# A wait ahead of every indirect transfer of the first layer

## The reference

```python
residual = x
xn = _layernorm(x, ln_g, ln_b)
abel = gelu(xn @ aw1 + ab1) @ aw2 + ab2                       # dense, hidden width 512
nonabel = _rotate(_moe(xn, gate_w, gate_b, ew1, eb1, ew2, eb2), gens)  # top 2 of 6 experts, width 256
gate = sigmoid(concat([abel, nonabel]) @ gc_w + gc_b)
return residual + abel * (1 - gate) + nonabel * gate
```

## Time and profile before

| what | value |
|---|---|
| median of 3 runs | 826.95 us (826.12 to 827.61) |
| the profiled execution's own time | 825.18 us |
| its span in the profile | 823.5 us |
| PE busy | 654.0 us, 79% |
| DVE busy | 500.6 us, 61% |
| ACT busy | 398.7 us, 48% |
| POOL busy | 388.6 us, 47% |
| TensorE's mean granted clock | 0.902 |

### The profile page before, as it was taken

One profiled execution on the slowest core, in us unless ns is written; L12 is line 12 of the kernel. 1 busy time (PEld: TensorE's weight loads), 2 busy tenths in 40 slices (PEclk: granted clock), 3 DMA queues, 4 the chain that ended last, 5 costly groups with the idle time before them and its releaser, 6 DMA issues.

```text
span 823.5 us, 19422 instructions
## 1 busy us (share of the span) xinstructions
PE 654.0 (79%) x6221; PEld 464.7 (56%) x6222; DVE 500.6 (61%) x1349; ACT 398.7 (48%) x1102; POOL 388.6 (47%) x523
## 2 busy tenths in 40 slices
PE   5978776742688208888956899999899999989894
PEld 3766555641587208756744355545599974444442
DVE  5787432730466006529885887878644457767784
ACT  3433231201344004447751667877644446766794
POOL 6352863067401750068630366753333327766682
PEclk9998886985799658999966999999999999999998
DMA  8990111011356324311100000000022211111110
GB/s 240 305 291 1 36 42 39 1 48 55 66 104 107 70 52 88 84 39 30 26 11 26 15 22 26 28 28 2 9 63 70 70 34 40 34 31 31 27 28 26
DMA packets 69465, 48.33 MB, mean 59 GB/s; under 512 B 8011, under 2 KB 63750, under 8 KB 69382
## 3 DMA queue, kind: packets, MB, share of 16 engines
q1 hardware_dynamic: 62332, 34.09, 16.6%
q0 software_dynamic: 6144, 12.63, 5.6%
q10 hardware_dynamic: 906, 0.55, 0.2%
HBM read 24.00 MB, written 23.24 MB: 57 GB/s over the span
## 4 chain that ended last, share of the span: by engine, by line
PE 47%; issue 14%; DVE 11%; POOL 10%; another core or an unknown queue 7%; DMA 6%; ACT 3%; SPq 0%; DVEq 0%; POOLq 0%; ACTq 0%
PE bank L1640 8%; DMA xg<-x_half 5%; PE bank L1599 4%; PE bank L1692 4%; PE bank L1701 4%; POOL vs L1550 4%; PE bank L1061 3%; PE bank L1625 3%; PE bank L1047 3%; POOL xn_all L1529 3%; PE bank L1026 2%; PE bank L1016 2%; PE bank L535 2%; PE bank L518 1%
## 5 line engine op out<-in xcount | busy, mean ns | idle before, releaser
L1760 ACT ACTIVATE pb<-bank,nmx 128x512 f32<-128x512 f32 x256 | 173.4, 690 | 65.8 <-DVE nmx L1891 65.5
L1891 DVE TENSOR_REDUCE nmx<-bank 128x2 f32<-128x1024 f32 x128 | 154.9, 1215 | 6.7 <-PE bank L1640 6.0
L1640 PE MATMUL bank<-qk 64*128 64x512 f32 x512 | 131.4, 623 | 8.1 <-ACT pb L1760 5.7
L1550 POOL TENSOR_TENSOR vs<-vt,rz 128x256 f32<-128x256 f32 x128 | 78.6, 616 | 119.4 <-DVE rz L1867 117.0
L1108 ACT ACTIVATE turns<-bank,cols 128x128 f32<-128x128 f32 x148 | 46.6, 365 | 111.9 <-PE bank L1016 49.2
L345 POOL DMA_INDIRECT x_half<-pool_xy,slot x64 | 62.1, 970 | 53.9 <-DVE slot L747 35.1
L1006 PE MATMUL bank<-ident,xg 128*128 128x128 f32 x74 | 24.0, 325 | 76.0 <-issue 47.8
L1640 PEld LDWEIGHTS bank<-qk 64*128 64x128 f32 x512 | 42.4, 185 | 63.7 <-ACT pb L1760 33.2
L1625 PEld LDWEIGHTS bank<-pb,vs 128*32 128x32 f32 x2048 | 54.3, 110 | 38.6 <-issue 22.9
L1625 PE MATMUL bank<-pb,vs 128*32 128x128 f32 x2048 | 69.9, 275 | 2.5 <-POOL vs L1550 2.2
L1216 DVE TENSOR_TENSOR ys<-bank,b2x 128x129 f32<-128x129 f32 x74 | 21.7, 294 | 64.4 <-remote 42.0
(11 more groups left out here) (252 smaller groups left out, 1380.1 us busy)
## 6 DMA issues: line engine op xcount, KB each, us to landing
y_half<-ys SPq DMA_DIRECT2D x74, 64.5 KB
x_half<-zero SPq DMA_DIRECT2D x2, 2368.0 KB, 21.0
xg<-x_half SPq DMA_DIRECT2D x74, 64.0 KB
x_sorted<-zero SPq DMA_DIRECT2D x1, 2496.0 KB, 19.0
xn_all<-x_sorted SPq DMA_DIRECT2D x39, 64.0 KB, 1.8
y_sorted<-xn_all SPq DMA_DIRECT2D x39, 64.0 KB, 1.6
x_all<-in_L_attn_x_dram SPq DMA_DIRECT2D x8, 256.0 KB, 6.0
w<-in_L_ffn_W_dram SPq DMA_DIRECT2D x1, 2048.0 KB, 11.1
```

What stands on the lines that cost most here:

```text
L1550: pool.tensor_tensor(vs[s][:, :, :], vt[bt % 2][:, n // 2 % TT, :, :].rearrange("p j d -> p (j d)") .unsqueeze(1).broadcast_to([P, 2, D]), ...
L1640: mm = pe.matmul(psum[score_banks(k) + ab], qk[bt % 2][half, 1, h, 2 * m:2 * m + 2, :].rearrange("p a k -> p (a k)"), qk[bt % 2][half, 0, ...
L1760: act.activation(pb[s + ab][:, :], psum[score_banks(k) + ab], ACT.Exp, bias=nmx[:, s + ab:s + ab + 1], scale=1.0, accum_out=zz[:, s + ab:s ...
L1891: dve.tensor_reduce(nmx[:, s:s + 2], banks[:, score_banks(k):score_banks(k) + 2, :], AX.X, ALU.max, negate=True).then_inc(n_mx, 1)
```

## The change

Each indirect transfer of the first layer gets a wait ahead of it, for the transfer issued before it on the same semaphore. Only the first scatter of each half and the very first gather have none.

```diff
             def scatter(g):
-                for slot_w in (slot1, slot2):
+                for w, slot_w in enumerate((slot1, slot2)):
+                    if g % NTH or w:
+                        pool.wait_ge(t_sc0[g // NTH], 16 * (g % NTH * 2 + w))
                     pool.indirect_dma_start(
                         out=x_half[g // NTH], out_offset=bass.IndirectOffsetOnAxis(ap=slot_w[:, g:g + 1], axis=0),
                         in_=xh[:, g, :], in_offset=None).then_inc(t_sc0[g // NTH], 16)
...
             def gather(g):
                 h = g // NTH
                 for w, slot_w in enumerate((slot1, slot2)):
+                    if w or g % TT:
+                        pool.wait_ge(f_yg[g // TT], 16 * (g % TT * 2 + w))
+                    elif g:
+                        pool.wait_ge(f_yg[g // TT - 1], 16 * 2 * TT)
                     pool.indirect_dma_start(
                         out=yg_half[h][:, g % NTH, w, :], out_offset=None, in_=y_half[h],
                         in_offset=bass.IndirectOffsetOnAxis(ap=slot_w[:, g:g + 1], axis=0)).then_inc(f_yg[g // TT], 16)
```

## The result

The changed kernel took 874.36 us (median of 3 runs, 870.49 to 876.55) against 826.95 us before. The ratio is 1.0567, with a 95% interval of 1.0506 to 1.0629: slower by 47 us. The forecast was 870 us with a range of 838 to 918.

The account below looks back on a forecast made before the run. Stalls under dense transfers bound the block stage for some 80 us; the waits make POOL the bound. +23.4 us before the first residual and +20 in mixing, on 825.18, give 868.6, so a median of 870; range 838 to 918.

Parts of the forecast that it names:

- Groups A, B and C: First rows of scatters on POOL, 8, 8 and 16 transfers: forecast to end at 101.8, 126.2 and 168.3 us.
- The period of a scatter: Time from one scatter's issue to the next on POOL: 2.63 us instead of 1.26, bounds 2.29 and 2.9.
- Group D: The 32 scatters of half 1 on POOL: forecast from 168.6 to 251.1 us, where they ended at 208.08.
- POOL finds half 0 stored: Ahead of the first gathers: blocks of half 0 done by about 225, so POOL's earlier 49 us wait goes.
- The gathers: POOL's gathers: 3.03 us each, 3.5 under block traffic; those of half 0 from about 257.8 to 359.3 us.
- The mixing stage: Passes after the first residual: 12.2 us with four gathers, up to 11.0 with two; +20 us in all.
- rival 2: Block stage: stalls stay while any transfer is under way, so blocks crawl longer; about 940 us, chance 0.12.
- Rival 1: POOL's transfers: landings are shorter and the change gains; break-even at a mean period of 2.50, perhaps 800 us; chance 0.10.
- Rival 3: POOL's waits find nothing to wait for, each transfer landing before the next issue ends; no change, chance 0.02.
- the lost block time would come back as nothing: Block stage: some 80 us lost to stalls give no gain, since ACT and DVE then wait for POOL.
- the second layer has no such wait over its scatters: Second layer, scatters standing between other work: no "remote" wait found on ACT or DVE.

Follow-up runs that it names:

- e3: Kernel before, plus a wait for all transfers under way ahead of every fourth transfer only; 761.83 us, ratio 0.9328.
- e10: Repeat on another occasion of the kernel before plus a wait for all transfers under way ahead of every fourth; 737.01 us, ratio 1.0237.
- e9: The changed kernel itself, measured again on another occasion beside the kernel before; 851.93 us, ratio 1.1871.
- e1: Kernel before plus only the waits of the scatters, the gathers dense as before; 825.08 us, ratio 1.0084.
- e4: Kernel before, plus a wait for all transfers under way ahead of every eighth transfer only; 794.14 us, ratio 0.9731.
- e5: Kernel before, but each transfer waits for the one before the last, so two may be under way; 727.18 us, ratio 1.0111.
- e8: Kernel before, transfers unchanged, but each block's expert number is a constant instead of read from the table; 715.02 us, ratio 0.9956.
- e6: Kernel before, plus a POOL operation of 1.04 us ahead of every fourth transfer, without waiting for a landing; 730.03 us, ratio 1.0138.

## Why the prediction was right

**The bound moved to POOL's chain, as step by step forecast.** Groups A, B and C ended within 0.8 us of the forecast (C at 168.4 for 168.3, A at 102.5 for 101.8). Group A starts 1.3 us later (83.73 for 82.40), which the forecast did not have, and the shorter period gave that back.

**The period of a scatter** was 2.49 us for my 2.63. I had taken SP's release (2.41) and added 0.22 for POOL's waking; a third of that would have done. The Trainium skill, "DMA: Bandwidth & Descriptors", Anatomy of one DMA (SWDGE path), gives about 2.0 us and the bytes at 436 GB/s for a transfer, from which I estimate 2.15 us for these 64 KB. The trace agrees with neither reading of it: from one issue to the next it is 2.49, from the end of the issue 1.53.

**Group D was the mis-sized term.** "Group D, 32 transfers: 168.6 to 251.1" took until 259.7. I had priced a gather under block traffic and forgotten that the scatters of D stand beside the blocks of half 0 too. The first four periods were 2.5 to 2.8 us, the twelve from 179 to 221 us 2.7 to 4.1 (3.5 in the mean), and the mean over D was 2.90 (31 periods in 90.0 us). That is 8.6 us.

**"POOL finds half 0 stored" was wrong.** It waited 5.08 us. The blocks of half 0 were not all "done by about 225": 34 had been computed at 223.6, and the stores of the last six stood behind the first load of half 1 in SP's order, which waits for D's last landing. I had read blocks as independent of the half that comes next.

**The gathers** came out at 2.8 us quiet for my 3.03. Beside the blocks they took 3.2 to 4.2 for my 3.5. The two nearly cancel: 99.7 us from the first to the end of the last of half 0 (271.31 to 370.99), for 101.5. The residual stood at 393.87 for 383.5: 8.6 of D and 5.1 of the wait, less some 3 of the gathers.

**The mixing stage** cost 16.9 us for my 20. Passes were 11.5, 11.5, 11.9, 11.2, 9.4, 11.2 and 10.3 us. I had 12.2 for those with four gathers; the waits of 2.07 in it measured 1.80 to 1.89, and one 2.45.

The errors add up to +10.3, -3.1 and -1.4 (the second layer): 43.4 forecast and 49.2 measured, on the spans. So the mechanism was right and the near hit is in part luck: D and the wait for half 0 were 13.7 us too short, and three gains that were not forecast took back 7.6 (3.1 in the gathers, 3.1 in the mixing stage, 1.4 in the second layer).

**The stalls went,** as the forecast assumed, and rival 2 is out: no "remote" wait between 82 and 400 us while one transfer at a time was under way, and 32 blocks in 46 us beside them. Rival 1, the gain, is out by its own point of break-even: the mean period would have had to be 2.50, and only the quiet scatters were there. Rival 3 is out by every row of POOL. The sum in rival 1 has a slip: at 2.29 us a transfer group C would end at 158.4, but the prediction has the slots of half 1 only at about 165, so the residual would stand at some 334 and not at 328.

That the lost block time would come back as nothing was the sharpest step, and the runs put a number on it. Where no stalls are to be won, the change costs 134 us; where they are, 47. So what it takes away is worth some 87 us, and the waits cost more than that. I read the difference as stalls, since no trace of the quick condition has one; the kernel before itself was not traced there. The forecast did not foresee this condition at all: in it the changed kernel's 852 would still lie in the range, but the loss of 43 us would have been a third of the true one. e3 shows that the waits need not cost more than they win: with a quarter of the waits the price falls to a seventh (19 us in e10 for 134 in e9), and of the 99 us between the conditions (817.90 less 718.45) only 25 stay (761.83 in e3 less 737.01 in e10). The 75 won less the 19 paid are the gain of 56 us that e3 showed.

One observation of the prediction was too narrow: that the second layer has no such wait over its scatters. Over its gathers, four close together, DVE has them in the kernel before also (three waits of 3.4 to 3.6 us). So short work between the transfers doesn't keep the stalls away, as I had inferred; a wait for the landing ahead of every transfer does.

## What to carry over

A wait behind every indirect transfer costs a landing each, here 1.23 us above the dense period of 1.26 for a scatter in a quiet memory, 1.5 for a gather, and up to 3.0 beside other transfers. Where the issuing engine has idle time behind the transfers the price is nearly hidden (the scatters, 7 us); where its own work stands behind them that work is late by the sum (the gathers, 40 us), and what the waits relieve elsewhere counts for nothing. Here one wait for every four bought three quarters of the relief for a seventh of the price. And a gain that rests on stalls which the profile can't name must be measured again beside the kernel before, on another occasion: here the same version gained 7% and lost 2%.

## What the runs showed that I had not expected

The kernel before has two conditions some 100 us apart: 815 to 828 us in 11 runs of two occasions, 715 to 726 us in 26 runs of two others. What sets them apart in the traces is the stalls of ACT and DVE: all six traces of the first kind have "remote" waits, the changed kernel's only in its second layer, and none of the eight of the second kind has one (the kernel before was not traced there; e9 is the changed kernel, and the second layer of all eight is untouched). They come only over dense rows of POOL's indirect transfers, in e3 from the third one on. In the rows of four most end 0.4 to 1.2 us after the last issue; in the rows of 32 some end within the row and the last ones 2 to 5 us after it. ACT was held up to 16.9 us at a time in e1, DVE up to 19.1 in the earlier trace rows, and an issue took 0.96 us with stalls and without. The Trainium skill, "SBUF — State Buffer", Who interferes with whom, knows one lock only, on ports that DVE and GpSimd share, with ACT sharing its ports with no engine. That lock would not explain ACT's waits, and the traces don't show what ACT and DVE wait for.

What decides which condition a run finds stays open. The chip doesn't settle it, since e1 to e4 and e5 to e8 ran on the same one, 17 minutes apart. Nor was it shown which step of ACT and DVE is held up, their reads of the expert's number or something else: e5, e6 and e8, made to tell that, met the condition without stalls, and so did the repeats of the last two. That DVE stands still also in phase 1 (L819), where its program has not yet come to the blocks and their table, and in the second layer, at copies out of PSUM (L1843 and L1852 of the kernel before), speaks against the table of the first layer as the only cause. No experiment tried it.
